# The third block of keys of each attention unit goes through DRAM, in two transfers of the sync engine

## What is computed

```
q = split_heads(x @ w_q); k, v = split_heads(text @ w_k), split_heads(text @ w_v)
k_ip, v_ip = split_heads(ip_h @ w_k_ip), split_heads(ip_h @ w_v_ip)
out = merge(sdpa(q, k, v)) + merge(sdpa(q, k_ip, v_ip, mask=mask_ip))
out = out @ w_out + b_out + x
```

## Time and profile before

| | us |
|---|---|
| median of 3 runs | 404.16 (402.7 to 404.22) |
| profiled execution, its own time | 404.16 |
| its span | 402.3 |
| TensorE busy | 393.6 |
| VectorE busy | 336.9 |
| GpSimd busy | 156.1 |
| ScalarE busy | 129.1 |

### The profile page before, as it was taken

How to read it: one execution, slowest core, us unless ns; L and a number is a source line. 1 busy time by engine, 2 the same in 40 slices (tenths; PEclk the granted TensorE clock), 3 DMA queues, 4 the chain that set the end, 5 groups by cost and what they waited for, 6 DMA issues and landing times.

```text
span 402.3 us, 10795 instructions
## 1 busy us (share of the span) xinstructions
PE 393.6 (98%) x4452; PEld 292.3 (73%) x4452; DVE 336.9 (84%) x458; ACT 129.1 (32%) x196; POOL 156.1 (39%) x128
## 2 busy tenths in 40 slices
PE   8899999999999999999999999999999999999995
PEld 7688868577777776777777767777777677776773
DVE  4559779898899998998998999999989999999503
ACT  5236334453333322432323322343223322321100
POOL 0336622687326433364226442462227532222200
PEclk9999999999999999999999999999999999999998
DMA  8999736576657454764457454664466544544555
GB/s 280 382 374 333 206 78 233 158 232 171 182 158 223 132 139 138 196 190 138 137 168 231 124 148 135 209 172 145 121 211 193 142 131 127 156 124 119 178 158 182
DMA packets 42849, 72.96 MB, mean 181 GB/s; under 512 B 10544, under 2 KB 10672, under 8 KB 42800
## 3 DMA queue, kind: packets, MB, share of 16 engines
q1 hardware_dynamic: 37680, 67.02, 54.6%
q10 hardware_dynamic: 5120, 5.25, 5.2%
HBM read 35.53 MB, written 10.49 MB: 114 GB/s over the span
## 4 chain that ended last, share of the span: by engine, by line
PE 86%; DVE 3%; SPq 3%; DMA 3%; ACT 2%; issue 1%; ACTq 1%; DVEq 0%
PE ps L637 63%; PE ps L682 9%; PE ps L668 9%; PE ps L714 3%; SPq L259 2%; DMA wk_raw<-in_w_k 2%; ACT prob L395 1%; PE ps L720 1%; ACTq L403 1%; DVE text_max L501 1%; DVE prob L507 1%; ACT q L391 1%; DMA out_tiles<-res 1%; SPq L279 1%; DMA prob_k<-prob_t 1%
## 5 line engine op out<-in xcount | busy, mean ns | idle before, releaser
L357 POOL TENSOR_TENSOR prob<-prob,rden 128x1104 f32<-128x1104 f32 x40 | 82.2, 2056 | 200.5 <-DVE rden L530 200.5
L395 ACT ACTIVATE prob<-prob 128x1232 f32<-128x1232 f32 x40 | 50.0, 1250 | 65.7 <-DVE prob L518 65.7
L537 DVE STREAM_TRANSPOSE prob_t<-prob 128x1536 f32<-128x1536 f32 x40 | 70.7, 1767 | 0.2 <-POOL prob L359 0.2
L501 DVE TENSOR_REDUCE text_max<-ps 128x16 f32<-128x1104 f32 x40 | 52.1, 1303 | 17.1 <-PE ps L668 16.2
L637 PE MATMUL ps<-x_hi,wq_hi 128*128 128x512 f32 x200 | 59.2, 418 | 0.1
L637 PEld LDWEIGHTS ps<-x_hi,wq_hi 128*128 128x128 f32 x200 | 34.6, 188 | 33.9 <-issue 28.1
L525 DVE TENSOR_REDUCE den<-prob 128x16 f32<-128x1104 f32 x40 | 50.6, 1265 | 7.3 <-ACT prob L395 7.2
L438 ACT ACTIVATE o_hi<-ps 128x512 fp32r<-128x512 f32 x40 | 23.7, 592 | 101.9 <-PE ps L682 98.1
L637 PE MATMUL ps<-o_hi,wo_hi 128*128 128x512 f32 x200 | 55.6, 392 | 0.0
L637 PE MATMUL ps<-o_hi,wo_lo 128*128 128x512 f32 x200 | 55.1, 389 | 0.0
L637 PE MATMUL ps<-o_lo,wo_hi 128*128 128x512 f32 x200 | 55.1, 389 | 0.0
(11 more groups left out here) (58 smaller groups left out, 346.4 us busy)
## 6 DMA issues: line engine op xcount, KB each, us to landing
prob_k<-prob_t SPq DMA_DIRECT2D x320, 64.0 KB
stage<-in_x SPq DMA_DIRECT2D x38, 256.0 KB, 3.0
res<-in_x SPq DMA_DIRECT2D x37, 256.0 KB
out_tiles<-res SPq DMA_DIRECT2D x37, 256.0 KB, 2.2
prob_k<-prob_t ACTq DMA_DIRECT2D x160, 32.0 KB
wki_raw<-in_w_k_ip SPq DMA_DIRECT2D x5, 512.0 KB, 7.0
wk_raw<-in_w_k SPq DMA_DIRECT2D x5, 512.0 KB, 6.7
wv_raw<-in_w_v SPq DMA_DIRECT2D x5, 512.0 KB, 8.9
```

The costliest lines, as they stand in the source:

```text
L357: nc.gpsimd.tensor_tensor(e[:, :, 0:TEXT], e[:, :, 0:TEXT], rden[:, par, 0, :].unsqueeze(2).to_broadcast([P, QT * HG, TEXT]), ALU.mult)
L395: nc.scalar.activation(prob[:, c % 2, :, 0:TOKENS], prob[:, c % 2, :, 0:TOKENS], ACT.Exp).then_inc(exp_done, 1)
L501: nc.vector.tensor_reduce(text_max[:, par, :, :], s[:, :, :, 0:TEXT], AX_X, ALU.max).then_inc(text_max_done, 1)
L537: nc.vector.transpose(prob_t[:, c % 2, :, :, :].rearrange("p k n r -> p n k r"), prob[:, c % 2, :, :].rearrange("p n (k r) -> p n k r", r= ...
```

## The change

The third block of keys of a unit is no longer moved by ScalarE. The sync engine writes the whole of that block, all 128 partitions of 2 KB, to a DRAM buffer (`rest_out`), one for each parity, ahead of its eight moves, and reads the needed 16 rows of each group of 32 back from there in one transfer (`rest_in`: 16 partitions of four pieces of 2 KB) behind them. `rest_in` waits for a semaphore of its own, `spilled`, which tells that the buffer has been written. `moved` now counts nine transfers for a unit in place of twelve. The turning on VectorE waits in addition for `spilled` of two units before.

```diff
+        spill = nc.dram_tensor("spill", (2, P, QT * HG * SQ), F32, kind="Internal").ap()
...
-            return 16 * QB * KB * (c // 2 + 1)
+            return 16 * (QB * (KB - 1) + 1) * (c // 2 + 1)
...
+            def rest_out(c):
+
+                sp.wait_ge(turned, c + 1)
+                if c >= 2:
+                    sp.wait_ge(moved[c % 2], moves(c - 2))
+                sp.dma_start(spill[c % 2], prob_t[:, c % 2, 2, :, :].rearrange("p n r -> p (n r)")).then_inc(spilled[c % 2], 16)
+
+            def rest_in(c):
+
+                sp.wait_ge(spilled[c % 2], 16 * (c // 2 + 1))
+                src = spill[c % 2].rearrange("(a k) e -> k a e", a=QB)[0:SQ // 2, :, :]
+                sp.dma_start(prob_k[2 * SQ:2 * SQ + SQ // 2, c % 2, :, :, :].rearrange("p a n r -> p a (n r)"),
+                             src).then_inc(moved[c % 2], 16)
...
+                rest_out(c)
                 for kb in range(2):
                     move(c, kb)
+                rest_in(c)
...
-            def move_rest(c):
-
-                act.wait_ge(turned, c + 1)
-                if c >= 2:
-                    act.wait_ge(o_made, c - 1)
-                for a in range(QB):
-                    act.dma_start(prob_k[2 * SQ:2 * SQ + SQ // 2, c % 2, a, :, :],
-                                  prob_t[SQ * a:SQ * a + SQ // 2, c % 2, 2, :, :]).then_inc(moved[c % 2], 16)
...
-                move_rest(c)
...
                     dve.wait_ge(moved[c % 2], moves(c - 2))
+                    dve.wait_ge(spilled[c % 2], 16 * (c // 2))
```

More of the change, by code:

```diff
@@ L168, in xattn_kernel @@
         turned = sem("turned")
+        spilled = [sem(f"spilled{k}") for k in range(2)]
         moved = [sem(f"moved{k}") for k in range(2)]
```

## The result

The changed kernel takes 438.65 us (median of 4 runs, 436.7 to 446.58) against 404.19 (median of 4): the ratio is **1.084, 95% interval 1.080 to 1.087**. The forecast was 426.0 us, range 410 to 438: the direction and the mechanism hold, the size is short by 13 us. (Ratios leave out runs more than 1.5% above the fastest of the same kernel: here the one at 446.58, without which the times are 436.7 to 439.1, and in the experiments 417.01 us of `after_residual_behind` and 965.29 us of the kernel before.) The profiled execution took 438.24 us, its span 436.4.

The account below looks back on a forecast made before the run. TensorE paces the middle at 8.9 us a unit; the sync queue would need 8.46 + 0.48 + 0.48 = 9.42 and take over, putting the last `make_o` 21.8 us later: 404.16 + 21.8 = 426.0 us, range 410 to 438.

Parts of the forecast that it names:

- The queue's own need of 8.46 us and its spare of 0.42: Sync queue, middle: a unit takes 8.88 us, of which 0.42 is waiting for the transpose, leaving 8.46 needed.
- Issue costs: Sync queue: the transfer out costs 0.48 us (0.37 to 0.63) a unit, the transfer back 0.63, gaps included.
- Give back 0.15, as the store then follows a DRAM transfer.: Sync queue, store behind the transfer back: its issue need not wait for the last move's, saving 0.15 us a unit.
- Bursts as long as before: Sync engine's eight moves: no faster without ScalarE issuing beside them; step of 0 us a unit.
- Behind it nothing changes: Kernel's end, after the last `make_o`: last output tiles' products, sums and stores stay as they were.
- The signs: Middle: no transpose waits, bursts 9.3 to 9.5 us apart, TensorE waiting about 0.5 at `make_o`, `spilled` never, ScalarE's busy time unchanged.
- The landing of the transfer back: `rest_in`, 128 KB from DRAM onto 16 rows: taken to land in 2.7 us, between bounds 2.04 and 3.1.
- The transfer out was taken for a store: `rest_out`, ahead of the moves: shaped like a store; stores land after 2.2 us, 4.3 at most, so `spilled` waits are hidden.
- rival 3: Way through DRAM slow: transfer out landing later than 5.5 us stalls `rest_in` and the queue; over 440 us; chance 0.06.
- Rival 1: Queue just fits: both transfers cost 0.42 us or less a unit, only the end pays +3.7; 408 us; chance 0.11.
- The Trainium skill's rule: Issuing from several engines saves only sequencer time, usually small beside the DMA; by it the sum would be that of rival 1.
- The early saving on ScalarE: Chain at 69.89 to 72.97 us: ScalarE's issues ahead of the w_out copies go, saving at most 0.9 us.

Follow-up runs that it names:

- after_residual_behind: Changed kernel with the residual load, which waits for the store's landing, issued behind the burst of moves; 411.8 us, ratio 1.018 to the kernel before.
- experiment 1: Kernel before plus one unread transfer of the third block out to DRAM per unit, ahead of the moves; 414.34 us, ratio 1.026.
- experiment 6: Kernel before with ScalarE's four third-block transfers issued by the sync engine behind its eight, directly within SBUF; 483.91 us, ratio 1.198.
- experiment 7: Residual load moved behind the burst or between its fourth and fifth move; changed kernel 411.8 and 405.87 us, kernel before 406.39 and 403.92 us.
- Experiments 2 and 3: Kernel before plus an unread 128 KB transfer in between moves and store: DRAM to 16 rows 426.93 us, to 32 rows 417.69, SBUF to 16 rows 454.94.
- experiment 4: Changed kernel with the transfer back (`rest_in`) issued behind the next store instead of ahead of it; 416.76 us, ratio 1.032 to the kernel before.
- before_extra_in: Kernel before plus one unread transfer per unit from DRAM onto 16 rows, between moves and store; 426.93 us, ratio 1.055.
- scalar_both: Changed kernel with `rest_out` and `rest_in` issued by ScalarE instead of the sync engine; 409.96 us, ratio 1.015 to the kernel before.
- extra_in_wide: Kernel before plus one unread 128 KB transfer per unit from DRAM onto 32 rows, between moves and store; 417.69 us, ratio 1.034.
- experiment 5: The run `scalar_both`: changed kernel with both new transfers issued by ScalarE instead of the sync engine; 409.96 us, ratio 1.015 to the kernel before.
- after_residual_mid: Changed kernel with the residual load issued between the fourth and fifth move of the burst; 405.87 us, ratio 1.005 to the kernel before.
- sync_twelve: The run of experiment 6: kernel before with ScalarE's four third-block transfers issued by the sync engine behind its eight; 483.91 us, ratio 1.198.

## Why the prediction was right, and where it was short

- *The queue's own need of 8.46 us and its spare of 0.42* held: with 0.5 us more it paces the kernel (experiment 1), with 2.5 more a unit is 11.0 (experiment 6), and with its idle filled the price is gone (experiment 7).
- *Issue costs* of 0.48 and 0.63 measured 0.47 and 0.63 where nothing stretched them. In the means they are 0.59 and 0.64.
- *"Give back 0.15, as the store then follows a DRAM transfer."* This is the step that failed. The store's issue did shrink, 0.58 to 0.43, but its landing is what the queue waits for, and that grew: +0.53 a unit in place of -0.15. Over 32 units the 0.68 are 22 us. Experiments 2 and 3 show the cause in the kernel before, the crowding of a transfer in on 16 rows; experiment 4 shows in the changed kernel that the landing is 2.3 again once `rest_in` isn't ahead of the store. The changed kernel was not tried with `rest_in` on more rows.
- *Bursts as long as before* failed the other way: 5.25 in place of 5.63, 12 us over 32 units. It is not ScalarE's absence. In `before_extra_in`, where ScalarE issues its four as before, bursts are 5.31; in `scalar_both`, where it issues two transfers, 5.56. Nor is it only that the queue sets the pace: bursts are 5.16 to 5.31 in the kernels with units of 9.5 us and more, but 5.59 and 5.63 with units of 9.25 and 9.10 (`extra_in_wide`, experiment 1), where the queue sets the pace too. What differs is where the stretched issue falls: of the moves in the 32 bursts 21 last over 0.8 us before and 9 after, which is 8 of the 12 us, and in the kernel after it falls also into the transfer out (1.42 us at most in place of 0.38) and the loads of x. The traces have a candidate for its cause: from 60 us on all 26 issues of the sync engine over 0.8 us in the kernel before, and all 19 in the kernel after, overlap a 16 KB packet of the queue that the page calls instruction (29 and 30 packets, a median of 10.4 and 12.0 us apart); of the other 385 issues before, 25 do. No run changed these packets, so what stretches an issue stays open.
- So a unit is 9.83 where 9.42 was forecast; 32 x 0.41 = 13 us, the whole shortfall. Burst 7's unit began at 96.85 (forecast 97.35), that of burst 39 at 411.48 (398.8), the last `make_o` at 420.96 (407.1), 35.7 us later than before. *"Behind it nothing changes"* was off by 1.6 us: from the last `make_o` to the end of the span there are 15.4 us where there were 17.0.
- *The signs.* `make_o` waits about 1 us a time (28.2 us in 29 places), not 0.5, as the queue's unit is 0.9 us over TensorE's and not 0.5. ScalarE's busy time is 132.8 us, 3.7 more than before, which I can't explain.
- *The landing of the transfer back*, taken as 2.7, is 2.9. The transfer out was taken for a store, with a landing of 2.2 us; it is 3.5 in the median, and the moves between hide it. `spilled` was waited for only in units 0, 1 and 3 (6.8 us, before the queue mattered), so rival 3 fell, except that experiment 5 shows its mechanism under the bulk loads.
- *Rival 1* (408 us) needed a queue that fits: that is what `after_residual_mid` made, and it came to 405.87. *The Trainium skill's rule* that several issuing engines save only a little sequencer time (DMA: Bandwidth & Descriptors) is not borne out here: in `sync_twelve` the same twelve transfers cost 80 us more on one engine than on two.
- The early saving on ScalarE (0.9 us at most) is seen: `make_o` of unit 5 ran at 87.8, before at 88.3.

## What to carry to other kernels

An engine that only issues transfers can be the bound, though it has no line among the busy ones: add its issues and the landings that it waits for in order, and hold the sum against the unit of the engine that seems to set the pace. Before moving transfers into such a queue, look for an idle wait in it and put the transfers that are ready ahead of what waits. A transfer onto few partitions delayed the landing of the store queued behind it here, so its price was not only its own issue.

## What the runs showed of the hardware that I had not expected

- The landing of a store (256 KB to DRAM) goes by the transfer ahead of it in the queue: 2.2 us behind moves of 64 KB, 2.5 behind 128 KB onto 32 rows, 3.0 onto 16 rows, 3.8 from 16 rows onto 16 rows within SBUF. Issued 0.62 us behind such a transfer of 128 KB, it landed 0.4 to 0.7 us after it.
- An issue's price goes by its predecessor as well as by what it issues. Behind a move between SBUF places it is 0.58 to 0.59 us for all kinds (the store, the transfer back, the residual in the middle, the next move). Behind a transfer to or from DRAM it is 0.38 for the transfer out, about 0.43 to 0.46 for a store or a load of x, and 0.51 for a move. After an idle wait it is 0.32 to 0.34 for a transfer to or from DRAM and 0.51 for a move.
- TensorE's granted clock, in the profiled run of the kernel after, stood at 2.4 GHz but for three stretches at 1.2 GHz: 3.4 us from 126.1, 3.4 from 235.3 and 6.8 from 399.1. TensorE had waited ahead of them: from 116 to 126 us it was busy for 8.91 us, from 225 to 235 for 8.60, and from 389 to 399 for 7.47. In the kernel before there was one such stretch, at 399.7, in the epilogue. The stage with the third of them, and a stage of `sync_twelve` (columns as in the earlier trace rows):

```profile
400.00:421.00 21.00, 17.64 (x77) 11.88 (x80) 4.48 (x5) 1.20 (x2) 1.75 (x2) 0.86 0.55 154
```

```profile
205.00:250.00 45.00, 41.21 (x412) 28.30 (x411) 33.07 (x44) 10.27 (x14) 12.99 (x12) 0.85 0.43 127
```

In `sync_twelve` the mean of the profiled run is 0.865 of 2.4 GHz, against 0.997 in the kernel before, but waiting doesn't explain all of that: it was at 0.85 from 20 to 60 us already, where TensorE was busy 40.00 us of 40.00. The products then last longer, and as the queue sets the pace, this costs the kernel nothing that shows: that run took 484.64 us, and the three others, with 0.943 to 0.947, took 480.48, 483.18 and 486.22.
